# Performer attention: the output rows of a head computed in pairs with shared releases, and a wait per quarter of the feature maps

## What is computed

```python
def _apply_kernel(x, orf):                     # orf: 256 x 64
    proj = einsum('bhld,md->bhlm', x, orf) / d_k ** 0.25
    norm = sum(x * x, axis=-1) / (2.0 * sqrt(d_k))
    return (exp(proj - norm) + EPS) / sqrt(m)
q_phi = _apply_kernel(q, orf); k_phi = _apply_kernel(k, orf)
kv   = einsum('bhlm,bhld->bhmd', k_phi, v)
ksum = sum(k_phi, axis=2)
num  = einsum('bhlm,bhmd->bhld', q_phi, kv)
den  = einsum('bhlm,bhm->bhl', q_phi, ksum)
out  = num / den[..., None]
```

## Time and profile before

| | us |
|---|---|
| median of 3 runs | 7830.36 |
| lowest and highest of the 3 | 7447.29, 7899.96 |
| the profiled execution (it is the one of 7447.29) | 7447.29 |
| its span on the slowest core | 7445.3 |
| spans of the 8 cores | 7419.3 to 7445.3 |
| stretch of the 16 heads of `attn_a` in it | about 195 to 1014 |

### The profile page before, as it was taken

How to read it: one execution, slowest core, us unless ns; L and a number is a source line. 1 busy time by engine, 2 the same in 40 slices (tenths; PEclk the granted TensorE clock), 3 DMA queues, 4 the chain that set the end, 5 groups by cost and what they waited for, 6 DMA issues and landing times.

```text
span 7445.3 us, 83252 instructions; the slowest of 8 cores (7419.3 to 7445.3 us)
## 1 busy us (share of the span) xinstructions
PE 5162.0 (69%) x21469; PEld 2064.1 (28%) x21856; DVE 2487.2 (33%) x5348; ACT 1405.8 (19%) x2392; POOL 260.7 (4%) x435
## 2 busy tenths in 40 slices
PE   2556554565564677999996874565564678999995
PEld 1222222111111333444442322111111333444442
DVE  3333325423323423222223455423323423222221
ACT  1221220243342101111111010243342101111110
POOL 0000000000000000000000000000000000000000
PEclk9556566666676788999998876666676789999998
DMA  3001022000103441222223022000103431222223
GB/s 81 4 6 18 6 38 68 12 10 11 21 11 67 95 68 23 35 35 45 35 35 66 14 32 62 9 10 11 22 11 68 95 68 23 35 44 37 35 35 91
DMA packets 278194, 277.59 MB, mean 37 GB/s; under 512 B 181649, under 2 KB 188177, under 8 KB 277778
## 3 DMA queue, kind: packets, MB, share of 16 engines
q0 software_dynamic: 84336, 162.75, 12.9%
q1 hardware_dynamic: 193442, 109.50, 6.0%
HBM read 287.73 MB, written 63.05 MB: 47 GB/s over the span
## 4 chain that ended last, share of the span: by engine, by line
PE 60%; DVE 12%; issue 9%; ACT 8%; DMA 5%; DVEq 2%; SPq 1%; ACTq 1%; another core or an unknown queue 0%; POOL 0%; POOLq 0%
PE PS L214 60%; ACT SCF L224 6%; DVE SCF L219 3%; DVE XNT L219 2%; DVEq L73 2%; DVE SM L219 2%; DVE SCB L219 2%; ACT SCA L224 1%; DVE SCA L219 1%; DVE STAT L219 1%; DMA sp_x<-R 1%; DMA SCA<-d_y 1%; DMA d_lo<-SCB 1%; SPq L78 1%; DMA STAT<-wrout 1%
## 5 line engine op out<-in xcount | busy, mean ns | idle before, releaser
L214 PE MATMUL PS<-XNT,WB 128*128 128x512 bf16 x9272 | 2062.1, 382 | 96.2 <-ACT SCA L224 52.0
L214 PEld LDWEIGHTS PS<-XNT,WB 128*128 128x128 bf16 x9472 | 932.3, 99 | 1219.4 <-issue 122.4
L214 PE MATMUL PS<-WB,SCA 128*128 128x512 bf16 x4766 | 1084.7, 387 | 240.8 <-DMA SCA<-d_y 150.6
L224 ACT ACTIVATE SCF<-PS,SM 128x512 bf16<-128x512 f32 (+3 forms) x1280 | 773.1, 622 | 1108.2 <-PE PS L214 1021.1
L214 PE MATMUL PS<-SCF,SCA 128*128 128x512 bf16 x1238 | 608.9, 492 | 391.3 <-DVE SCF L219 191.9
L224 ACT ACTIVATE SCA<-PS 128x512 bf16<-128x512 f32 x768 | 444.7, 595 | 2238.0 <-PE PS L214 1997.8
L219 DVE TENSOR_TENSOR SCA<-SCA,PS 128x512 bf16<-128x512 bf16 x512 | 352.3, 688 | 1430.4 <-PE PS L214 1326.2
L214 PEld LDWEIGHTS PS<-WB,SCA 128*128 128x128 bf16 x4864 | 479.9, 99 | 836.8 <-issue 293.7
L214 PE MATMUL PS<-XNT,SCA 128*128 128x512 bf16 x1270 | 635.9, 515 | 43.2 <-ACT SCF L224 19.7
L219 DVE SCALAR_TENSOR_TENSOR R<-PS,STAT,R 128x512 f32<-128x512 f32 x448 | 315.7, 746 | 507.8 <-PE PS L214 507.8
L214 PE MATMUL PS<-IDENTB,SCF 128*128 128x128 bf16 x768 | 97.3, 305 | 505.8 <-DVE SCF L219 505.8
(11 more groups left out here) (122 smaller groups left out, 2682.9 us busy)
## 6 DMA issues: line engine op xcount, KB each, us to landing
WB<-wg_r POOLq DMA_DIRECT2D x28, 1024.0 KB, 13.0
WB<-wu_r POOLq DMA_DIRECT2D x28, 1024.0 KB, 23.6
WB<-wd_r POOLq DMA_DIRECT2D x28, 1024.0 KB, 13.0
sp_x<-R SPq DMA_DIRECT2D x8, 2048.0 KB, 17.2
R<-sp_x POOLq DMA_DIRECT2D x8, 2048.0 KB, 28.1
R<-x SPq DMA_DIRECT2D x4, 2048.0 KB
SCA<-XNT SPq DMA_DIRECT2D x32, 256.0 KB, 2.9
d_yraw<-SCF POOLq DMA_DIRECT2D x128, 64.0 KB, 1.9
```

Source lines behind the costliest of these rows:

```text
L214: return e.matmul(out_ap, lhsT, rhs, start=start, stop=stop, tile_position=tp)
L224: return getattr(e, name)(*a, **kw)
```

## The change

Two edits, both in the steps of one head.

The Q features (step 5): the loops are exchanged, so that the two feature halves of one block of rows come right behind each other. The banks still alternate between 6 and 7. The value of `s_ac` is noted after each block of rows, in `v_eq_lb`.

The output rows (step 6): the 16 steps become 8 pairs. A pair's six matmuls (banks 0 and 1) come first, then both reciprocals into two columns of `SM0`, one drain, both multiplies, one drain, and then both banks are released together. A step waits for the exponentials of its own block of rows, `v_eq_lb[l // 4]`, and no longer for all.

```diff
-                for mc2 in range(2):
-                    for lb in range(4):
-                        bk = 6 + (lb % 2)
+                v_eq_lb = {}
+                for lb in range(4):
+                    for mc2 in range(2):
+                        bk = 6 + (mc2 % 2)
...
                         p.release(f"ps{bk}", s_ac)
+                    v_eq_lb[lb] = s_ac.v
                 v_eq = s_ac.v
 
-                for l in range(NT):
-                    bk = l % 2
-                    bank = PS[bk]
-                    w0 = p.use(f"ps{bk}") + [(s_ac, v_eq), (s_dv, v_c), (s_ac, v_g)]
-                    for mc2 in range(2):
-                        mm(bank[:, 0:65], ...)
-                    mm(bank[:, 0:65], SCF[0:1, 128 * l:128 * l + 128],
-                       SCA[0:1, 16642:16707], start=False, stop=True)
-                    vm = s_mm.v
-                    v_op("reciprocal", SM0[:, 0:1], bank[:, 64:65], wait=[(s_mm, vm)])
-                    p.drain("vector")
-                    v_op("tensor_scalar_mul",
-                         SCB[:, 6144 + 128 * l + 64 * hh:6144 + 128 * l + 64 * hh + 64],
-                         bank[:, 0:64], SM0[:, 0:1], wait=p.use("pairout"))
-                    p.drain("vector")
-                    p.release(f"ps{bk}", s_dv)
+                for lp in range(8):
+                    vms = []
+                    for j in range(2):
+                        l = 2 * lp + j
+                        bank = PS[j]
+                        w0 = (p.use(f"ps{j}") +
+                              [(s_ac, v_eq_lb[l // 4]), (s_dv, v_c), (s_ac, v_g)])
+                        for mc2 in range(2):
+                            mm(bank[:, 0:65], ...)
+                        mm(bank[:, 0:65], SCF[0:1, 128 * l:128 * l + 128],
+                           SCA[0:1, 16642:16707], start=False, stop=True)
+                        vms.append(s_mm.v)
+                    v_op("reciprocal", SM0[:, 0:1], PS[0][:, 64:65],
+                         wait=[(s_mm, vms[0])])
+                    v_op("reciprocal", SM0[:, 1:2], PS[1][:, 64:65],
+                         wait=[(s_mm, vms[1])])
+                    p.drain("vector")
+                    for j in range(2):
+                        l = 2 * lp + j
+                        v_op("tensor_scalar_mul",
+                             SCB[:, 6144 + 128 * l + 64 * hh:
+                                 6144 + 128 * l + 64 * hh + 64],
+                             PS[j][:, 0:64], SM0[:, j:j + 1],
+                             wait=(p.use("pairout") if j == 0 else ()))
+                    p.drain("vector")
+                    p.release("ps0", s_dv)
+                    p.release("ps1", s_dv)
```

More of the change, by code:

```diff
@@ new lines, in phase_attn_a @@
+                for lp in range(8):
[6 more added lines that the diff above has]
+                        for mc2 in range(2):
+                            mm(bank[:, 0:65],
+                               SCA[:, eqo + 2048 * mc2 + 128 * l:
+                                   eqo + 2048 * mc2 + 128 * l + 128],
+                               SCA[:, kvo + 65 * mc2:kvo + 65 * mc2 + 65],
+                               start=(mc2 == 0), stop=False,
+                               wait=(w0 if mc2 == 0 else ()))
+                        mm(bank[:, 0:65], SCF[0:1, 128 * l:128 * l + 128],
[5 more added lines that the diff above has]
+                         wait=[(s_mm, vms[1])])
+                    p.drain("vector")
+                    for j in range(2):
[5 more added lines that the diff above has]
+                             wait=(p.use("pairout") if j == 0 else ()))
```

## The result

The changed kernel takes 1.0069 times the time of the kernel before (95% interval 1.0055 to 1.0083): some 51 us more, and within the 2% that count as the same. The forecast ratio was 7503 / 7447.3 = 1.0075. The time itself came out at a median of 7623.9 us over 13 executions (7487.34 to 8129.02), outside the forecast range of 7465 to 7555; the kernel before had a median of 7626.55 over its 13.

What follows compares the result with a forecast made beforehand. The prediction took the changed stretch as bound by the round trip between TensorE and VectorE. Pairs cost 4.5 us a head, quarters gain 1.0, over 16 heads 56 us: 7447.3 + 56 = 7503.3 us, range 7465 to 7555.

Steps and rivals of the forecast that it cites:

- The level: Whole kernel: an execution like the profiled one of 7447.3 us, so 7503.3 us, with 20 us either way between executions.
- The direction and the size: Whole kernel: slower by 56 us, or 0.75%, as the output rows in pairs cost more than the quarters bring.
- TensorE's idle time before these matmuls: Step 6, a sign to look for: waiting on VectorE grows from 90.1 to about 160 us.
- The round trip: Step 6: the two banks' trips no longer overlap, so a pair takes 2.30 us against 1.62.
- The chained multiplies: Step 6, VectorE: second multiply taken at 0.24 us; by the skill's rule 0.28, the change some 5 us dearer.
- The waits of the second step: Step 6, TensorE: four waits ahead of a pair's second step, taken as hidden in the matmuls' 0.87 us.
- The quarters: Start of step 6: it can begin when step 5's eighth matmul ends, gaining 1.0 us a head (0.7 to 1.05).
- First and second heads: Step 6 in a head pair: 4.60 us more for the first head, 4.36 for the second, before the quarters' gain.
- the clock rival: Projections after a head: more idle step 6 keeps them at low clock, 12 us more each, 7587 us; chance 0.04.
- The new waiting is cheap: Step 6, rival: the way back shrinks from 0.47 to 0.2 us, a cycle of 2.03, 7467 us; chance 0.06.
- The quarters bring nothing: Start of step 6, rival: something else holds it, the 16 us gain is missing, 7519 us; chance 0.05.
- The pairs pay: Step 6, rival: VectorE's stream alone limits, a pair takes 1.18 us instead of 1.62, 7375 us; chance 0.03.

Runs made afterwards that it cites:

- e4: The changed kernel with its pairs alternating between banks 0, 1 and banks 2, 3; measured 0.9887 of the kernel before.
- e5: The changed kernel with TensorE's waits of step 6 put only where they first matter; measured 1.0009 of the kernel before.
- e1: The kernel before with only the exchanged loops and the wait per quarter, old output steps kept; measured 0.9985 of the kernel before.
- e7: Against the kernel before: four output steps per bank with one reciprocal and one multiply, four banks, quarter waits, short wait lists; measured 0.9846.
- e6: The kernel before with the waits of step 6 for l > 0 cut to the bank's release; measured 1.0061 of the kernel before.

## Why the prediction was right in its mechanism and wrong in its time

**The level, wrong.** The step that failed is the sentence "I forecast an execution like the profiled one", and with it the 20 us either way for differences between executions. What the runs showed in its place: the median of 13 executions was 7623.9 us for the changed kernel and 7626.55 for the kernel before, and only six of the 13 of the changed kernel lay in the forecast range. Two of the three times shown stood at 7830 and 7900, and the trace at hand was of the third. A range for "the time" had to span the level of such executions or say that it held for the difference only; mine did neither. That the two medians are alike already says that this level has nothing to do with the edit, and the changed kernel's own profile shows it. Core 1 and core 4 in the same execution, in the stretch of the 16 heads and at the end of the kernel; core 1 first:

```profile
190.00:1060.00 870.00, 474.05 (x2624) 195.10 (x2622) 273.26 (x933) 185.83 (x337) 5.94 (x8) 0.59 0.06 10
...
6000.00:7465.00 1465.00, 1372.80 (x5588) 583.80 (x5587) 347.73 (x631) 143.24 (x249) 31.22 (x42) 0.86 0.19 35
```

```profile
190.00:1060.00 870.00, 473.23 (x2624) 194.73 (x2621) 273.57 (x933) 185.71 (x337) 5.92 (x8) 0.59 0.05 10
...
6000.00:7465.00 1465.00, 1295.79 (x5882) 579.62 (x5879) 372.95 (x666) 145.52 (x252) 36.41 (x46) 0.94 0.25 47
```

Up to 1060 us the cores are alike: the last multiply of the 16 heads ends at 1064.53 on core 1 and at 1063.71 on core 4. The 156 us between their spans come later, for the most part where TensorE is nearly always busy at the full clock: there the granted clock is 0.86 instead of 0.94, and fewer matmuls fit into the same window. A window of 100 us shows it more sharply, core 1 and then core 4:

```profile
7200.00:7300.00 100.00, 100.00 (x383) 41.43 (x381) 16.50 (x24) 14.34 (x24) 0.00 (x0) 0.81 0.00 1
```

```profile
7200.00:7300.00 100.00, 100.00 (x465) 45.30 (x463) 24.76 (x36) 12.04 (x21) 1.49 (x2) 1.00 0.12 22
```

Core 1 is granted 0.81, between its low and its full clock, for some 820 us in all, all of them after 6030 us; core 4 never is. By my estimate 820 us at 0.81 instead of 1.00 lose some 155 us, which is the whole difference. What lowers the clock there in some executions no run here settles.

**The direction and the size, right.** 51 us against 56, and TensorE's idle time before these matmuls came to 156.1 us where 160 were forecast. Part of the closeness is luck: some 4.5 of the 51 us come from longer projections, which the prediction had put at nothing. By the steps:

- *The round trip.* Forecast 2.30 us a pair, measured 2.26 to 2.29. Every term is in the trace: matmuls 0.88 (in later pairs 0.91), 0.11, 0.17, the drain 0.16, two multiplies 0.48, way back 0.46. The term that was sized a little high is the second multiply, 0.24 where 0.20 was measured.
- *The chained multiplies.* The prediction set a rule of the Trainium skill (VectorE: DVE Perf Modes, section "The DRAIN you can't avoid") beside this term, and carried it further than the page does. The page compares copies with a semaphore after each of them and after the last alone, and finds no difference. It gives no price for a drain instruction, and it adds that a next operation which nothing holds starts earlier. The trace agrees with that addition: two chained multiplies took 0.48 us where two isolated ones take 0.57. And an edit that takes drain instructions away does save VectorE time: each left a gap of 0.16 us, and those ahead of the multiplies fell from 39.6 to 18.3 us. On two banks the kernel gained nothing by it; on four (e4) it did.
- *The waits of the second step.* I took them as hidden in the 0.87 us. Kernel e5 shows that some 0.08 of it are three of these waits.
- *The quarters.* Forecast 1.0 us a head, measured 1.0 in the first heads of e1. That the gain is bounded by the eighth matmul, whatever the loops' order, held.
- *First and second heads.* Forecast 3.6 and 3.36 us net, measured 3.1 and 3.5. In the first there are the shorter cycle, and the single gaps that I had let stand in both kernels: step 6 takes 17.7 us in the mean where I had 17.93, and before it took 13.5 in the mean where I had subtracted 13.33. The second contains a term that I had denied: the projections got longer. Over the six between heads that have 64 matmuls the mean on core 4 is 16.1 us against 15.5 (the seventh has 192 matmuls, 51.1 against 50.3). This is the clock rival in small. The windows of 1 us over the start of a projection on core 4, before and after, show it:

```profile
813.50:814.50 1.00, 1.00 (x4) 0.29 (x2) 0.00 (x0) 0.00 (x0) 0.00 (x0) 0.50 0.19 45
814.50:815.50 1.00, 1.00 (x4) 0.37 (x3) 0.00 (x0) 0.00 (x0) 0.00 (x0) 0.57 0.98 215
815.50:816.50 1.00, 1.00 (x6) 0.41 (x5) 0.59 (x1) 0.00 (x0) 0.00 (x0) 1.00 0.95 215
```

```profile
853.70:854.70 1.00, 1.00 (x4) 0.43 (x3) 0.25 (x1) 0.00 (x0) 0.00 (x0) 0.50 0.97 217
854.70:855.70 1.00, 1.00 (x5) 0.36 (x4) 0.50 (x1) 0.00 (x0) 0.00 (x0) 0.77 0.44 101
855.70:856.70 1.00, 1.00 (x6) 0.49 (x5) 0.05 (x1) 0.00 (x0) 0.00 (x0) 1.00 0.00 0
```

Before, the projection started at 812.51 and the clock rose to its full level by 815.4; after, it started at 850.75 and the clock rose at about 855.2, 4.4 us in instead of 2.9. That is 1.5 us more at half speed, which costs half of it, here 0.8 us (16.14 against 15.38), and in the seven projections together some 4.5 us. The price I had given, 12 us for each, was that of a clock that never rises. The reason I had given for it, a more idle step 6, is not borne out: e7 has the least idle step 6 of all, and its projections take 15.6 to 16.3 us on core 4, also longer than before in the mean; and e1, whose step 6 is the old one, has 15.3 to 16.9. Why the kernel before has its clock back soonest stays open, and so does whether the edit as such is the cause.

**The rivals.** "The new waiting is cheap" needed a shorter way back; e5 shows what would have made it so, and that the diff didn't do it. "The quarters bring nothing" fell with e1. "The pairs pay" was wrong for this kernel for the reason given, no second set of banks, and e4 confirms that reason by supplying one.

## What to carry to other kernels

Where two engines hand small tiles to and fro, count the round trip, not the busy time: with two buffers, batching two tiles per handshake makes one buffer of them, and every saved drain is paid back as a wait. Batching pays once there is a second set of buffers (e4). The fastest kernel, 1.5% under the one before, puts four outputs into one bank, but on four banks and with short wait lists; whether that would also pay on two banks no run shows. Look also at the wait lists: waits that were satisfied long ago stand in the queue behind the one that blocks and lengthen each trip.

## What the runs showed of the hardware

- Three wait instructions on TensorE that are already satisfied cost 0.32 us behind one that blocks (e5: from 0.47 to 0.15 us), so by estimate 0.1 us each. Three ahead of the second step cost 0.08 together. In e6, where VectorE was nearly the limit, leaving them out brought only 0.07 us a pair.
- A VectorE `tensor_tensor` from a PSUM bank over four blocks of 64 columns, with the second operand repeated by a step of 0, took 0.42 us for 128x256; four separate multiplies of 128x64 took 4 x 0.28.
- The same 64 matmuls of a projection take 15.4 us in one kernel and 16.1 in another, where the granted clock rises 2.9 and 4.4 us after their start.
- In the profiled execution of the changed kernel core 1 is granted 0.81 for some 820 us of its dense stretches, while core 4, with the same program, stays at 1.00 there and ends 156 us sooner.
